# Row maxima of a causal softmax: the mask added inside the maximum on VectorE, denominators spread by a shuffle, and the work lists ordered anew

## The reference

```python
scores = jnp.einsum('bhqd,bhkd->bhqk', q, k) / math.sqrt(Hd)
scores = scores + causal[None, None]          # -inf above the diagonal
attn = jax.nn.softmax(scores, axis=-1)
out = jnp.einsum('bhqk,bhkd->bhqd', attn, v)
```

## Time and profile before

| what | us |
|---|---|
| median of 3 runs | 1397.1 (1396.12 to 1402.0) |
| span of the profiled execution | 1418.7 |
| TensorE busy, share of the span | 1338.4, 94% |
| VectorE | 1126.6, 79% |
| ScalarE | 949.1, 67% |
| GpSimd | 698.8, 49% |
| chain that ended last: TensorE, VectorE, ScalarE, transfers | 60%, 20%, 6%, 4% |

### The profile page before, as it was taken

How to read it: one execution, slowest core, us unless ns; L and a number is a source line. 1 busy time by engine, 2 the same in 40 slices (tenths; PEclk the granted TensorE clock), 3 DMA queues, 4 the chain that set the end, 5 groups by cost and what they waited for, 6 DMA issues and landing times.

```text
span 1418.7 us, 32580 instructions
## 1 busy us (share of the span) xinstructions
PE 1338.4 (94%) x12308; PEld 1091.0 (77%) x12308; DVE 1126.6 (79%) x2294; ACT 949.1 (67%) x2607; POOL 698.8 (49%) x806
## 2 busy tenths in 40 slices
PE   6999999778999999999999999999999998999997
PEld 3544446667888879888889798888888987789896
DVE  4587436889979788969798879697888897988886
ACT  3105751476777768777778678677687777787774
POOL 8012222337754565464745655556555557555431
PEclk9979999889999999999999999999999999999999
DMA  9900001212101121131311311312212114111000
GB/s 320 191 5 1 4 1 45 75 40 72 44 25 37 31 87 35 31 88 33 85 37 32 91 31 39 83 30 76 46 32 68 43 31 116 38 31 31 24 2 31
DMA packets 59507, 76.68 MB, mean 54 GB/s; under 512 B 6200, under 2 KB 46776, under 8 KB 59352
## 3 DMA queue, kind: packets, MB, share of 16 engines
q1 hardware_dynamic: 54616, 60.31, 16.7%
q0 software_dynamic: 4736, 14.29, 3.6%
HBM read 62.92 MB, written 11.67 MB: 53 GB/s over the span
## 4 chain that ended last, share of the span: by engine, by line
PE 60%; DVE 20%; ACT 6%; issue 5%; DMA 4%; POOL 3%; another core or an unknown queue 1%; SPq 0%; POOLq 0%; DVEq 0%; ACTq 0%
PE ps L930 10%; PE ps L1313 6%; DVE yv L1644 4%; PE ps L977 4%; DMA RC<-crow 3%; PE ps L1218 3%; DVE yk L1644 3%; PE ps L1266 2%; PE ps L1295 2%; PE ps L1228 2%; PE ps L1231 2%; PE ps L985 2%; PE ps L1282 2%; PE ps L1267 2%; PE ps L1291 2%
## 5 line engine op out<-in xcount | busy, mean ns | idle before, releaser
L1988 ACT ACTIVATE XY<-ps 128x512 f16<-128x512 f32 x384 | 221.2, 598 | 88.6 <-PE ps L1231 75.2
L1734 DVE TENSOR_TENSOR ZL<-ps,cst 128x256 f16<-128x256 f32 x384 | 155.0, 418 | 47.4 <-PE ps L1218 40.8
L1644 DVE SCALAR_TENSOR_TENSOR yv<-ps,cw,yv 128x511 f32<-128x511 f32 (+2 forms) x192 | 143.3, 746 | 7.0 <-ACT yv L1925 2.3
L930 PE MATMUL ps<-XH,WVh 128*128 128x256 f32 (+1 forms) x384 | 133.9, 349 | 1.2 <-ACT hT L1973 1.2
L1313 PE MATMUL ps<-WO,OGT 128*128 128x256 f32 x512 | 126.8, 391 | 3.2 <-DVE OGT L1806 2.9
L930 PE MATMUL ps<-XH,WVl 128*128 128x256 f32 (+1 forms) x384 | 123.5, 322 | 0.0
L930 PE MATMUL ps<-XL,WVh 128*128 128x256 f32 (+1 forms) x384 | 123.3, 321 | 0.0
L2181 POOL TENSOR_TENSOR RC<-RC,dec 128x512 f32<-128x512 f32 x64 | 69.3, 1083 | 100.8 <-DMA RC<-crow 100.6
L1228 PE MATMUL ps<-ZL,XY 128*128 128x64 f16 x1536 | 105.7, 193 | 8.1 <-DVE ZL L1734 4.4
L1218 PE MATMUL ps<-XY,LT 128*128 128x64 f16 x1536 | 101.1, 193 | 12.9 <-ACT XY L1988 11.1
L1218 PEld LDWEIGHTS ps<-XY,LT 128*128 128x128 f16 x1536 | 80.0, 98 | 42.4 <-issue 20.1
(11 more groups left out here) (305 smaller groups left out, 4122.0 us busy)
## 6 DMA issues: line engine op xcount, KB each, us to landing
RC<-crow SPq DMA_DIRECT2D x128, 128.0 KB
WV<-in_WV SPq DMA_DIRECT2D x16, 512.0 KB, 3.6
WK<-in_WK SPq DMA_DIRECT2D x16, 256.0 KB, 2.7
WO<-in_WO SPq DMA_DIRECT2D x16, 256.0 KB, 2.8
rows_out<-st SPq DMA_DIRECT2D x7, 512.0 KB
KS<-spread SPq DMA_DIRECT2D x12, 256.0 KB, 12.1
QS<-spread SPq DMA_DIRECT2D x12, 256.0 KB, 16.5
w<-in_w SPq DMA_DIRECT2D x4, 512.0 KB, 8.7
```

Of the source, the lines that this page charges most:

```text
L930: m = pe.matmul(o, a, b, start=c + k == 0, stop=c == 1 and k == 2)
L1644: m = dve.scalar_tensor_tensor(out=dst[:, k:512], in0=ps[:, bk, 0:512 - k], scalar=cw[:, h, j, 3 - k:4 - k], in1=dst[:, k:512], op0=ALU.mu ...
L1734: leave(dve.tensor_tensor(half(ZL[:, k - 2], k, 0), p, lv(k), ALU.mult), "a", u, k)
L1988: leave(act.activation(changed(u, k), ps[:, bank("b", u, k), :].rearrange("p (c n t) -> p c n t", c=2, t=1 << (k - 1)), ACT.Copy), "b", u, k)
```

## The change

Four things. The mask matmuls of `p1` go; instead VectorE runs, for each head, one instruction that adds a constant tile `ahead` (bf16, -1e30 above the diagonal in its last 128 columns and zero in the others) to the scores, writes the sum back over them in PSUM, and gives the row maximum. The selection matmul of `ov` goes; VectorE copies `OT` by a shuffle in which every lane of a block of 32 takes lane 16, waits for it, and takes the reciprocal in place in SBUF. GpSimd makes `ahead` where it made the identity and `high`. All ranks, `GRAIN`, `DELAY` and many weights of the planner have new numbers, so every list is ordered anew, those of layer 1 among them.

```diff
-C_ID, C_SEL, C_U, C_ONE, C_X1, C_Y1, C_LV = 0, 128, 256, 384, 512, 640, 768
+C_ID, C_U, C_ONE, C_X1, C_Y1, C_LV = 0, 128, 256, 384, 512, 640
...
-    "p1": {"DVE": 26.78, "PE": -1.261}, "pl": {"POOL": -95.917}, "pre": {"ACT": -110.761, "DVE": -90.125},
+    "p1": {"DVE": 244.972, "PE": -191.722}, "pl": {"POOL": -420.379}, "pre": {"ACT": 789.397, "DVE": -1001.002},
...
-    GRAIN = 0.09700
-    DELAY = {"PE": 0.22, "DVE": 0.18, "ACT": 0.24, "POOL": 0.19, "SP": 0.1, "DMA": 0.1}
+    GRAIN = 0.05128
+    DELAY = {"PE": 0.21, "DVE": 0.16, "ACT": 0.19, "POOL": 0.13, "SP": 0.1, "DMA": 0.1}
...
-                P.add(x, -200 + 20 * b, ("PE", 0.36 + 0.055 * (i + 1), (("stack", b), "SP")),
-                      ("DVE", 0.1 + 0.27 * (i + 1)), takes=2, gives=x)
+                P.add(x, -200 + 20 * b, ("PE", 0.05 + 0.06 * (i + 1), (("stack", b), "SP")),
+                      ("DVE", 0.2 + 0.27 * (i + 1)), takes=2, gives=x)
...
-            P.add(("ov", b, g), rank, ("PE", 0.86, (("oc", b, g), "ACT")), ("DVE", 3.36, am), takes=True, gives=("ov", b, g))
+            P.add(("ov", b, g), rank, ("DVE", 3.9, (("oc", b, g), "ACT"), am))
...
-        P.add(x, rank[k], ("PE", 1.48, (("fWK", h), "POOL"), *(ready(b) if h < 3 else ())), ("ACT", 0.58, to), ("DVE", 1.99),
+        P.add(x, rank[k], ("PE", 1.48, (("fWK", h), "POOL"), *(ready(b) if h < 3 else ())), ("ACT", 0.58, to), ("DVE", 2.22),
...
+        ahead = sb("ahead", [128, 512], BF16, scope=sc)
...
                     for hh in range(2):
                         p0 = 64 * hh
-                        pe.matmul(ps[:, bk + hh, 0:L],
-                                  QS[p0:p0 + 64, g, 512 * b + 128 * i:512 * b + 128 * i + 128],
-                                  KS[p0:p0 + 64, g, 512 * b:512 * b + L], start=True, stop=False, skip_group_check=True)
-                    w.wait_ge(s_c0, 4)
-                    for hh in range(2):
-                        m = pe.matmul(ps[:, bk + hh, L - 128:L], idh, high, start=False, stop=True,
-                                      skip_group_check=True)
+                        m = pe.matmul(ps[:, bk + hh, 0:L],
+                                      QS[p0:p0 + 64, g, 512 * b + 128 * i:512 * b + 128 * i + 128],
+                                      KS[p0:p0 + 64, g, 512 * b:512 * b + L], start=True, stop=True)
                     signal(m, *x)
...
-                elif what == "ov":
-                    b, g = x[1:]
-                    bk = enter(*x)
-                    w.wait_ge(*done("pv", b, g, 0))
-                    m = pe.matmul(ps[:, bk, :], cst[:, C_SEL:C_SEL + 128], OT[:, g % 2, :], start=True, stop=True)
-                    signal(m, *x)
...
-                    o = Mp[:, 4 * b + i, 4 * g:4 * g + 4].rearrange("p (h k) -> p h k", k=2)[:, :, 0]
-                    leave(dve.tensor_reduce(o, ps[:, bk:bk + 2, 0:L], AX.X, ALU.max), *x)
+                    w.wait_ge(s_c0, 3)
+                    for hh in range(2):
+                        at, s_ = 4 * g + 2 * hh, ps[:, bk + hh, 0:L]
+                        m = dve.tensor_tensor_reduce(out=s_, in0=s_, in1=ahead[:, 512 - L:512], scale=1.0, scalar=-3e38,
+                                                     op0=ALU.add, op1=ALU.max, accum_out=Mp[:, 4 * b + i, at:at + 1])
+                    leave(m, *x)
...
-                    w.wait_ge(*full(*x))
-                    if 4 * b + g > 1:
-                        w.wait_ge(s_aT, 4 * b + g - 1)
-                    leave(dve.reciprocal(rB[:, g % 2, :], ps[:, bank(*x), :]), *x)
+                    n = 4 * b + g
+                    w.wait_ge(*done("pv", b, g, 0))
+                    if n > 1:
+                        w.wait_ge(s_aT, n - 1)
+                    dve.stream_shuffle(rB[:, g % 2, :], OT[:, g % 2, :], [16] * 32).then_inc(s_den, 1)
+                    w.wait_ge(s_den, n + 1)
+                    dve.reciprocal(rB[:, g % 2, :], rB[:, g % 2, :]).then_inc(s_rec, 1)
...
-            w.wait_ge(d_cst, 16)
-            pool.tensor_copy(idh, ident).then_inc(s_c0, 1)
-            pool.memset(high, -1e30).then_inc(s_c0, 1)
-            w.wait_ge(s_c0, 3)
-            pool.affine_select(out=high, in_=high, compare_op=ALU.is_gt, fill=0.0, base=0, pattern=[[1, 128]],
+            pool.memset(ahead[:], -1e30).then_inc(s_c0, 1)
+            w.wait_ge(s_c0, 2)
+            pool.affine_select(out=ahead[:], in_=ahead[:], compare_op=ALU.is_gt, fill=0.0, base=-384, pattern=[[1, 512]],
                                channel_multiplier=-1).then_inc(s_c0, 1)
...
-                    w.wait_ge(*done("ov", b, g))
+                    w.wait_ge(s_rec, 4 * b + g + 1)
```

More of the change, by code:

```diff
@@ L37, in constants @@
     c[:, C_ID:C_ID + 128] = np.eye(128)
-    sel = c[:, C_SEL:C_SEL + 128]
-    for h in range(4):
-        sel[32 * h + 16, 32 * h:32 * h + 32] = 1.0
     c[:, C_U:C_U + 128] = i[:, None] <= i[None, :]
@@ new lines @@
+    "gram": {"DVE": 93.65, "PE": -0.066}, "gt": {"ACT": -975.504, "PE": -875.11},
+    "kn": {"ACT": 147.251, "PE": -2.992, "POOL": 219.195}, "kns": {"ACT": -31.332},
+    "ln1": {"ACT": 88.955, "DVE": 511.437, "PE": -142.273}, "max": {"SP": 373.594}, "mk": {"POOL": 507.23},
+    "nr2": {"DVE": 259.564}, "nrm": {"DVE": -220.649, "POOL": 909.749}, "oc": {"ACT": 101.646}, "on": {"ACT": 31.215},
+    "op": {"DVE": -414.956, "PE": 357.19}, "ot": {"DVE": 351.82, "PE": -421.911}, "ov": {"DVE": 3.296},
@@ L186, in plan_experts0 @@
         x, y = ("exg", e, b), ("exv", e, b)
-        P.add(x, rank, ("PE", 1.81), ("ACT", 0.62, *old), takes=True, gives=x)
+        P.add(x, rank, ("PE", 1.81), ("ACT", 0.49, *old), takes=True, gives=x)
         P.add(y, rank + 1, ("PE", 1.81), ("DVE", 0.6, (x, "ACT")), takes=True, gives=y)
@@ L231, in plan_rows0 @@
         b = n // 4
-        P.add(("op", n), -90 + 60 * b, ("PE", 1.72, *[(("am", b, g), "POOL") for g in range(4)]),
+        P.add(("op", n), -90 + 60 * b, ("PE", 1.8, *[(("am", b, g), "POOL") for g in range(4)]),
               ("DVE", 1.2, (("g0", b), "ACT"), (("op", n - 1), "DVE") if n else None), takes=True, gives=("op", n))
@@ L266, in plan_prologue @@
         P.add(("gt", b), -9, ("PE", 1.48, *ready(b), (("spg",), "POOL")), ("ACT", 0.6), takes=True, gives=("gt", b))
-        P.add(("gg", b), -9, ("PE", 0.44, (("gt", b), "ACT")), ("DVE", 0.45), takes=True, gives=("gg", b))
+        P.add(("gg", b), -9, ("PE", 0.46, (("gt", b), "ACT")), ("DVE", 0.45), takes=True, gives=("gg", b))
     both = [(("gg", b), "DVE") for b in range(2)]
@@ L272, in plan_prologue @@
     P.add(("pre", 3), -9, ("ACT", 1.7, (("pre", 2), "DVE")), ("DVE", 0.9))
-    P.add(("cum",), -9, ("PE", 1.0, (("pre", 3), "DVE")), takes=True)
-    P.add(("crow",), -9, ("PE", 0.44, (("pre", 3), "DVE")), ("ACT", 0.5), ("SP", 2.5), takes=True)
+    P.add(("cum",), -9, ("PE", 1.7, (("pre", 3), "DVE")), takes=True)
+    P.add(("crow",), -9, ("PE", 0.85, (("pre", 3), "DVE")), ("ACT", 0.5), ("SP", 2.5), takes=True)
     P.parts[("crow",), "ACT"].gives = ("crow",)
@@ L313, in plan_values @@
             to = (("KS", 4 * (h - 1) + 2 * q + 1, b), "DVE") if h else None
[L314 removed]
+            P.add(x, rank[4 + 4 * q + b], ("PE", 0.46, (("cv", h, 0, b), "DVE"), (("cv", h, 1, b), "DVE")),
                   ("ACT", 0.49, to), takes=True, gives=x)
@@ L335, in plan_inverse @@
     P.add(("row", u), rank - 1, ("SP", 2.5, (("crow",), "SP"), earlier(RCS, "dec", "ACT")))
-    P.add(("dec", u), rank, ("POOL", 2.1, (("row", u), "SP"), (("pre", 4), "DVE")),
+    P.add(("dec", u), rank, ("POOL", 1.82, (("row", u), "SP"), (("pre", 4), "DVE")),
           ("ACT", 0.53, earlier(1, "pt", "DVE"), (("cc", 1), "POOL")))
@@ L402, in plan_routed @@
 def plan_routed(P):
-    P.add(("cnt",), -3.5, ("PE", 3.5, (("top", 2), "DVE")), ("DVE", 11.0, (("xr", 1), "SP")), takes=True, gives=("cnt",))
+    P.add(("cnt",), -3.5, ("PE", 6.0, (("top", 2), "DVE")), ("DVE", 11.7, (("xr", 1), "SP")), takes=True, gives=("cnt",))
     P.add(("slot",), -3.5, ("PE", 1.2, (("cnt",), "DVE")), ("DVE", 0.2), takes=True, gives=("slot",))
@@ L593, in build @@
         cw = sb("cw", [128, HK, 4, 4])
-        cb = sb("cb", [128, 2, 128], BF16)
-        idh, high = cb[:, 0, :], cb[:, 1, :]
         WK, WKl = twins("WK", "WKl", [128, 2, 2, 256])
```

64 lines of the change are left out of this document (29 added, 35 removed), and 22 rows, old and new, of the table RANK.

## The result

The changed kernel takes 1402.2 us (median; 1396.7 to 1408.9) where the kernel before takes 1399.4 beside it: a ratio of 1.0023, 95% interval 1.0012 to 1.0033. A second measurement on another chip gave 1.0027 (1.0010 to 1.0044). Some 3 us are lost where 11.7 were forecast to be won. The chips differ, and with them the absolute times: the kernel before takes about 1399 us on one kind and 1418 to 1421 on the other, and the trace of before is from the second kind, the first trace of after from the first. Landmarks are compared within one kind, or in layer 0, where both kinds agree (a second trace of the changed kernel, on the slower kind, has its last product with wo at 247.1 us and the first at 247.2).

A forecast was written before the change was run, and what follows sets the result against it. TensorE was taken to bound the kernel, with VectorE taking over in batch 0's maxima. From 1397.1 us, -6.7 - 7.6 + 5.5 + 1.1 - 4 = -11.7 gave 1385; own range 1377 to 1393, 8 in 10 within 1368 to 1404.

The forecast's parts named there:

- Price of the fused group: Layer 0's row maxima on VectorE: 3.7 us per group of four tiles; +5.5 us in batch 0, +1.1 in batch 1.
- The bound above it: Upper bound for the fused instruction in layer 0: twice the price, 6.3 us per group, from rows taking 483 and 891 ns.
- Price of the shuffle: Layer 0's spreading on VectorE: 0.7 us per shuffle plus 0.1 for the wait, 6.4 us in all, none on the path.
- Work taken from TensorE is worth its full time: Layer 0, 46 to 242 us: TensorE has no gap, so removed work counts fully except where another engine takes over.
- Masks: Mask products leave TensorE in layer 0: only batch 1's 32 pairs count, at 0.21 us each, 6.7 us off the path.
- selection product: Selection product leaves TensorE in layer 0: 8 groups of heads at 0.95 us, 7.6 us off the path.
- Parts 1 to 4: Layer 0's instruction changes: masks -6.7, selection product -7.6, fused maxima +5.5 and +1.1, shuffle nothing on the path.
- The end of layer 0: Sign that the forecast holds: the stretch 46 to 242 us ends 7 to 9 us earlier.
- The lists, -4: New weights, delays and ranks reorder all lists; only layer 1's 48.6 us of TensorE idle can move: -4, range 16 either way.
- signs of being wrong: Group over 4.3 us; layer 0's end moving under 3 or over 15 us; layer 1 moving more than layer 0.
- slower by the lists of layer 1: Rival, chance 0.10: TensorE's idle time in layer 1 grows by a third, 16 us, giving 1405 us.
- The gap filled: Rival, chance 0.20: expert products fill TensorE's 11 us free during batch 0's maxima, layer 1 gains 8; 1370 us.

The follow-up runs named there:

- ops_old_lists: The changed kernel's instructions with the ranks, grain, delays and weights of the kernel before (spreading's weight new), all lists made anew; 1.0048 of the kernel before.
- after_again: The changed kernel itself, unedited, measured and traced a second time on the slower kind of chip; 1.0027 of the kernel before.
- fused_only: The kernel before with its mask products and reductions replaced by the fused maxima, selection product kept, every list unchanged; 1.0019 of the kernel before.

## Why the prediction was wrong

The forecast was -11.7 us; the measured change is about +3.5 (the mean of the two measurements). By the steps:

- **Price of the fused group: right.** 3.7 forecast, 3.61 measured; one operation per 0.25, 0.35 to 0.38, 0.51 and 0.65 us for 128 to 512 columns, where 0.27, 0.40, 0.53 and 0.66 stood in the sum. Its effect, +5.5 and +1.1, was measured as +5.9 to +7.1. The accumulator's read is a second instruction of 142 ns, overlapped, so it costs 0.06 and not 0.14. The Trainium skill's page "VectorE: DVE Perf Modes" says in "Two Vector instructions with no wait between them" that such an operation is two instructions; the trace agrees. The bound above it rested on a misreading: the 891 ns of the earlier trace rows are the mean of four durations from 478 to 1631, so these rows do not tie a doubled price to where an operand lies.
- **Price of the shuffle: right, its place in part wrong.** 0.7 forecast, 731 ns measured. "Nothing on the path" failed at the last group, where no expert product was left to cover it: shuffle, reciprocal and scaling stand in a wait of 6.5 us. The shuffle is 0.72 of these.
- **"Work taken from TensorE is worth its full time": the first step that failed.** Masks -6.7 forecast, -3.3 to -4.5 measured; selection product -7.6 forecast, -3.0 with the order kept (with 8 of its columns left) and +3.1 with it made anew. Parts 1 to 4 were to give -7.7. In exactly the old order they give about nothing (+2.7 and -3.0, each by itself), and +6.7 where the old ranks make the lists anew. That TensorE was busy without a gap did not mean that it set the pace everywhere: with 19.5 us less work its last product with wo comes at the same time. How this comes about is argued, not shown: expert products fill TensorE while attention's own chain, through VectorE and ScalarE, is nearly as long, and taking work out of the filled engine uncovers that chain. 7 more table loads (9.0 us on ScalarE) and 18 us more work on VectorE in 112 to 242 may lengthen it; the low clock may take its part.
- **The end of layer 0: right by luck.** The forecast had it 7.7 us earlier (by its signs, 7 to 9). Layer 0 is handed over 9.6 us earlier and brings 7 us of time, but from the order of its lists, not from the work taken off TensorE.
- **The lists, -4: the second step that failed.** Changed kernel less ops_old_lists is 1.0027 - 1.0048 = -0.21%, 3 us, near the -4 by luck. It is made of -13.6, nearly all in layer 0, and +10.6 in layer 1. The forecast gave the lists one term, a share of TensorE's idle time of layer 1, and saw neither. Of its signs of being wrong, the last came true: layer 1 moved by more than layer 0 (+10.6 against -7). TensorE's idle time in 260 to 1380 us, 51.4 in after_again against 48.6, stayed within the bounds of the forecast and showed little of the loss. The rival *slower by the lists of layer 1* had the mechanism and nearly its size (16), with a chance of 0.10.
- **The gap filled.** The rival came true in layer 0: expert products did move between the maxima of batch 0 (clock 0.97). It did not bring its 11 us; expert products were missing later, under the last groups.
- **The clock.** The low level moved: 73 to 93 us before, 90 to 105, 158 to 167 and 234 to 242 after. Keeping it high in batch 0 by a filler brought nothing, so the low level of that stretch is not what costs there; its share of the rest stays open, and by the executions' mean clocks it could be as large as the losses of the kernels with the old ranks.

So three things stand: the instructions in the old order bring about nothing instead of 7.7 us; layer 0 gains 7 us with its new lists; and layer 1's new lists lose 10.6, through the fetches of the decay rows. Shown is that this loss goes when the fetches go. Whether it is their latency on the chain or their bytes was not separated, though taking seven eighths off the experts' larger gathers brought only 2 to 3 us and left the rows' share of the chain at 6.4%. Why the new ranks place the rows worse was not tried; the planner's 2.5 for a step that takes 5 is a candidate. Nor were the seven table loads priced by themselves.

## What to carry to other kernels

An engine that is busy all the time may be filled rather than limiting: before work is taken from it at full price, look at what fills it, and where the chain goes that the filler now covers. Cut a change that moves orders on all engines into instructions and lists per stage, and cross them; here two parts of 10 us and more hid in a sum of 3. When one piece of work leaves a planner, write out the old order for the comparison: ranks that stay the same do not keep the lists (the same shuffle was worth -3.0 us in the old order and +3.1 in the one made anew). A planner's sum of end times cannot see a step that it prices too low: put its price for every transfer beside the trace's landing time.

## What the runs showed of the hardware

- A fused addition and maximum over PSUM, written back over its source with the maximum accumulated, takes 0.65 us start to start for 512 columns and 0.25 for 128; the accumulator's read (142 ns) overlaps what follows. A stream shuffle of 128x512 takes 731 ns.
- A full TensorE did not always have the high clock: from 73 to 93 us of before it is busy 19.9 of 20 us, and the granted clock is 0.50 (1.2 GHz). With one more small product per tile it stayed at 1.00 through the maxima (28.00 us busy of 28 in 65 to 93 us, against 17.55 at 0.61 in fused_only). What made the difference was not tested.
- Among executions of the kernel before on one chip, 0.001 more mean granted clock went with 0.6 to 1.1 us less time (five chips, 11 to 31 executions each). Which of the two follows from the other was not tested.
- Two kinds of chip ran the same kernels 1.5% apart, with layer 0 alike to 0.2 us: the changed kernel's TensorE is busy 318.2 us in 400 to 740 on the slower kind and 329.2 on the other. What waits longer there was not followed up.
